# A graph kernel whose first sweep closes its rows with fixed weights and turns the results on VectorE

## The chip, the cores and the metric

One core of a Trainium2 chip. The time is what the device takes for one run of the program, in microseconds (us). TensorE (PE in the profile) multiplies, VectorE (DVE) adds and transposes, ScalarE (ACT) applies tanh and square root, GpSimd (POOL) and SyncE (SP) mostly issue transfers.

## What is computed

`adj` is a dense 8192 x 8192 float32 matrix, `x` is 8192 x 64. Four layers follow one another, each `x = x + layer(relu(layernorm(x)))`; the first has two hops, so that `adj` is multiplied five times:

```python
# layer 0, two hops: sweeps 1 and 2
for k in range(2):
    h = tanh(concatenate([adj @ h, h], axis=1) @ W[k])
# layer 1: sweep 3        adj @ (h @ weight) + bias
# layer 2: sweep 4        adj @ (h * (u >= 0.1) / 0.9)
# layer 3: sweep 5        concatenate([h, adj @ h / (deg + 1)]) @ W.T,  deg = sum(adj, axis=1)
```

The change is about layer 0. There `h` enters each hop twice: through `adj @ h` and, as the row's own features, beside it. The tanh of hop 1 is what hop 2 sweeps over, and is also hop 2's own features.

## The kernel before, in words

**Blocks and sweeps.** `adj` is cut into 16 x 16 blocks of 512 x 512 (1 MB each). A sweep makes, for each of the 16 rows i of blocks, the sum over j of block (i, j) times the features of nodes j. Since five sweeps would read the matrix five times, most blocks are used for two sweeps at one load: block (i, j) serves sweep s for row i and, as the features of nodes j for sweep s + 1 are already there, sweep s + 1 for row i too. Odd sweeps sum in partitions 0 to 63 (`row.half` 0), even ones in 64 to 127; `two_products` (L747) multiplies for both, `one_product` (L720) for one, splitting the 512 nodes of the row into two halves of 256 columns that stand in the two halves of the partitions. In the lists, sweep 1 goes down from row 0 to row 15; row i takes its blocks j > i and then j = i singly ("single"), and j = i - 2 and i - 1 as "double" at its end. Further, as soon as the features of nodes i - 1 exist for sweep 2, the blocks (k, i - 1) of all rows k > i + 1 are taken as "early" groups between the single blocks of row i. In the kernel before they start after the third single block of a row (after the fourth in row 1); where a row has too few, those left over stand behind its last single block. Rows 1 to 6 end with one more block of sweep 2 ("late"). Sweep 2 goes up from row 15 to row 0, and begins with a few late blocks before its short rows.

**The order of work** is one list, `PLAN`, written by `make_plan` (L122): "block", "first" and "doubles" (VectorE takes the sums of the single and double blocks from PSUM), "turn" (a row's own features are brought from nodes by partition to features by partition), "post" (a row is closed), "added" and "added_both" (a late or early group is added to `partial`). Every engine walks through the same list in order and does its part, with semaphores between them. SyncE loads blocks through a ring of 8 in the order of the list.

**Closing a row ("post").** `stack` holds, by features, 64 partitions of sums and 64 of own features, for 512 nodes. In `post` (L782) TensorE multiplies it with the 128 x 64 weights in `w_stack`: 8 products, in each of which 64 nodes of `stack` are the fixed operand and the 64 columns of the weights are streamed (L814). The results in `natural` have nodes by partition. ScalarE's tanh (L909) writes them in sweep 1 straight into `operand`, which is what sweep 2 multiplies with, and in sweep 2 into `tanh_out`, from which VectorE's `finish` makes the next layer's features, square root on ScalarE (L853) and operand (L1158) among it. In sweep 1 the post of row i - 1 stands after row i's second single block (after its only one in row 15).

**Turns.** In sweeps 1, 2 and 5 VectorE's `turn_in_squares` (L1011) transposes own features from `operand` into `stack` with 8 transposes of 32 partitions x 128 (L1028). Row 15 of sweep 2 is turned by TensorE (L779).

**Sums.** `take_first` (L1051) and `take_doubles` (L1084) bring a row's sums into `stack` (L1074, L1093); in sweep 1 `take_doubles` then also adds the other sweep's half to `partial` (L1009). In sweeps 2 to 4 that half is saved by a copy on ScalarE (L893) at "doubles". The next row but one that uses a sum bank waits for these.

**Degrees.** VectorE adds up `adj` for the row sums `deg`: two additions of 128 x 1024 for each block in `DEGREE_BLOCKS` (L989, L990; the first block of a row has one, L986) and a fold of three instructions at the end of a row (L994, L997, L1001). In sweep 1 all single blocks of rows 9 to 15 are among them, of rows 0 to 8 only the diagonal one, and the double blocks of rows 1 and 2; in sweep 2 the double blocks of rows 0 to 8. A ring slot is free only when its block has been added (L693).

Of the kernel before, what the change touches and what calls it, by code (L numbers as in the profile page):

```python
# [36 lines left out]
F = 64  # L37
P = 128
BLOCK = 512
NB = N // BLOCK  # L40
TPB = BLOCK // P
SQUARE = 32
# [58 lines left out]
ROW_OF = {(row.sweep, row.i): row for row in ROWS}  # L101


class Block:


# [4 lines left out]
def make_plan():  # L111
# [36 lines left out]
    def row_of(row, post_at, hoisted=False, between=None):  # L148


        n_single = 0 if hoisted else len(row.single)
        total = n_single + len(row.double)
        before = [("post", ROWS[row.r - 1])] if row.r % NB or row.sweep == SWEEPS else []
        if row.double:
            post_at = min(post_at, total - 1)
        at = {n: [] for n in range(total + 1)}
        if n_single == 0:
            at[0].append(("first", row))
        if row.own:
            at[min(1, n_single)].append(("turn", row))  # L160
        at[min(post_at, total)] += before
        for n in range(1, total + 1):
            at[n] += between(row.i, n) if between else []
        if row.sweep == 4 and row.i == DEGREES_AT:
            at[min(2, total)].append(("degree", row))
        if n_single:
            at[n_single].insert(0, ("first", row))
        if row.double:
            at[total].append(("doubles", row))
            if n_single:  # L170
                blocks(row, row.single, "single", {n: at[n] for n in range(n_single)})
            blocks(row, row.double, "double", {n - n_single: at[n] for n in range(n_single, total + 1)})
        else:
            blocks(row, row.single, "single", at)

    def upwards(sweep, between=None):
# [30 lines left out]
        for i in range(NB - 2, -1, -1):  # L207
            row = ROW_OF[sweep, i]
            if i >= NB - 4:

                plan.append(("first", row))
                turning = [("turn", row)] if row.own else []
                if i == NB - 2:
                    plan.extend(turning)
                if i < NB - 2 and fills[NB - i]:
                    takings = fill_with(fills[NB - i], False)
                    plan.append(("post", ROWS[row.r - 1]))
                    plan.extend(takings)
                    plan.extend(turning)
                    if i == NB - 3:  # L220
                        fill_with(fills[NB - i + 1])
                    blocks(row, row.double, "double")
                else:
                    blocks(row, row.double, "double", {1: [("post", ROWS[row.r - 1])] if i < NB - 2 else []})
                plan.append(("doubles", row))
            else:
                row_of(row, 1, between=between)
# [8 lines left out]
    for row in ROWS[:NB]:  # L236
        groups = [(k, [row.i - 1]) for k in range(row.i + 2, NB)] if row.i else []
        at_first = min(1, len(row.single) - 1)
        begin = 3 if row.i == 1 else 2
        starts = [min(begin + c, len(row.single) - 1) for c in range(len(groups))]  # L240
        for n, j in enumerate(row.single):
            plan.append(("block", Block(count[0], row, j, "single", n == 0, n == len(row.single) - 1)))
            count[0] += 1
            if n == (at_first if row.r else NB // 2):
                if row.r:
                    plan.append(("post", ROWS[row.r - 1]))
                plan.append(("turn", row))
# [202 lines left out]

def rows_in_squares(r):

    return sum(row.own and not turned_by_tensor(row) for row in ROWS[: r + 1])


def added_to(row):
# [71 lines left out]
def gnn_kernel(nc, adj, x, w_both, w_own, bias, u, identity, ones, out):  # L528
# [5 lines left out]
    with ctx:  # L534
# [93 lines left out]
        tanh_ready = sem("tanh_ready")  # L628
        sd_ready = sem("sd_ready")

        weights_cleared = sem("weights_cleared")

        def data_of(b):
# [25 lines left out]
        def wait_operand(wait_ge, sweep, j):  # L659
# [1 line left out]
            if sweep == 1:  # L661
                wait_ge(first_ready, j * TPB // GROUP + 1)
            elif sweep == 2:
                wait_ge(tanh_ready, ROW_OF[1, j].r + 1)
            else:
                wait_ge(norm_ready, ROW_OF[sweep - 1, j].r + 1 - NB)

# [40 lines left out]
        def _(pe):  # L708
# [73 lines left out]
            def post(row):  # L782
# [11 lines left out]
                    wait_new(later_consts, 16 * LATER_CONSTS)  # L794
                if turned_by_tensor(row):
                    wait_new(own_ready, rows_with_own(row.r))
                elif row.own:
                    wait_new(squares_ready, rows_in_squares(row.r))
                if row.r >= 2:
# [3 lines left out]
                    else:  # L803
                        wait_new(natural_taken, before.r + 1 - 2 * NB)
                acc = natural[row.r % 2]
                stacked = partial[:, row.i, :] if row.sweep == SWEEPS else stack[:, row.r % 2, :]
                for t in range(TPB):
                    if row is ROWS[-1] and t == TPB // 2:
                        last.then_inc(half_posted, 1)
                        wait_new(first_taken, rows_with_first(row.r))  # L810
# [35 lines left out]
        def _(act):  # L846
            deviations = [0]

            def deviation(n, slot):
# [2 lines left out]
                act.wait_ge(var_ready, deviations[0])  # L852
                nc.scalar.activation(sd[:, slot, 0:n], moments[:, slot, 0:n, 1], ACT.Sqrt, bias=eps[:, 0:1]).then_inc(sd_ready, 1)  # L853

            def scale_own(row):

                wait_operand(act.wait_ge, row.sweep, row.i)
# [25 lines left out]
            for g in range(2, NGROUPS):  # L883
                deviation(GROUP, g % 2)
            for what, row in PLAN:
                if what in ("block", "added", "added_both"):
                    continue
                slot = row.r % 2
                if what == "doubles" and row.sweep > 1:

                    act.wait_ge(blocks_used, used(row, "double"))
                    other = half_of(1 - row.half)
                    nc.scalar.copy(partial[other, row.i, :], double_acc[slot][other, :]).then_inc(partial_saved, 1)  # L893
                elif what == "scale" or what == "turn" and row.sweep == SWEEPS and row is not ROWS[-1]:
                    scale_own(row)
                elif what == "turn" and turned_by_tensor(row):
# [5 lines left out]
                elif what == "post":  # L902
                    if row.r == CONSTS_AT:
                        load_constants()
                    if row.sweep <= 2:
                        act.wait_ge(posted, posts(row.r))
                        got = natural[slot][:, 0:TPB * F].rearrange("p (t f) -> p t f", t=TPB)
                        to = operand[:, tiles(row.i), F:2 * F] if row.sweep == 1 else tanh_out[:, slot]
                        nc.scalar.activation(to, got, ACT.Tanh).then_inc(tanh_ready, 1)  # L909
                    if row.sweep in (2, 3, 4):  # L910
                        deviation(TPB, 0)
                    if row.sweep == SWEEPS:
# [14 lines left out]
        def _(dve):  # L927
# [111 lines left out]
            def turn_back(row):  # L1039
# [8 lines left out]
                last.then_inc(turned_back, 1)  # L1048
                dve.wait_ge(turned_back, rows_turned_back(row.r))

            def take_first(row):  # L1051


# [25 lines left out]
            def take_doubles(row):  # L1079
# [4 lines left out]
                    dve.wait_ge(first_taken, rows_with_first(row.r))  # L1084
                    before = stack[part, row.r % 2, :]
                else:
                    wait_stack(row)
                    wait_partial(dve.wait_ge, row)
                    if added_to(row):
                        dve.wait_ge(added_taken, added_to(row))  # L1090
                    dve.wait_ge(blocks_used, used(row, "double"))
                    before = partial[part, row.i, :]
                last = nc.vector.tensor_tensor(stack[part, row.r % 2, :], got[part, :], before, ALU.add)  # L1093
                last.then_inc(sums_ready, 1)
                if row.sweep == 1:
                    add_to(partial[other, row.i, :], got[other, :], ("doubles", row.r, row.sweep + 1) in FRESH)\
# [90 lines left out]
            for what, of in PLAN:  # L1187
# [7 lines left out]
                elif what == "first":  # L1195
                    take_first(of)
                    if of.r == 2 * NB:
                        make_folding()
                elif what == "doubles":
                    take_doubles(of)  # L1200
                elif what == "added":
# [48 lines left out]
```

## Time and profile before

| | |
|---|---|
| median of 3 runs | 2269.01 us (2268.98 to 2269.06) |
| the profiled execution | 2268.98 us |
| its span | 2267.2 us |
| PE, DVE, ACT busy | 2241.6, 1253.2, 116.4 us |
| share of PE in the chain that ended last | 97% |
| adjacency loads | 780 of 1 MB |
| granted TensorE clock | full in every slice |

The span is the time from the first to the last instruction of the profiled execution; 1.78 us of its time lie outside. Instructions are named by line and engine; a busy share of PE is modelled, since matmuls are pipelined, and a group's duration reaches beyond the start of the next by its drain. So PE's work is best read from start to start. One product in float32 shows as two matmul records with a weight load each: a single block is 16 of them with 256 columns, a double block 16 with 512.

### The profile page before, as it was taken

Reading aid. Unit: us, or ns where it says so; the run is one execution under the profiler, and the core shown is the slowest. Engines: PE = TensorE matmul, PEld = TensorE weight load, DVE = VectorE, ACT = ScalarE, POOL = GpSimd, SP = SyncE. Lnnn points to the kernel's source line nnn. Section 1 sums busy time; section 2 is a strip of 40 time slices with the busy share of each in tenths; the row PEclk is TensorE's granted clock in tenths of the full one; section 3 lists DMA queues with packets and bytes.
Section 4 is the critical chain, followed back from the end, with each engine's and each line's share of the span. In section 5 each row is a group of like instructions: output and inputs, shape, how many; then the busy total and the mean of one; then the engine's idle time right before and its main releaser. Section 6 shows DMA issues by size and latency. Waiting matters only on the chain.

```text
span 2267.2 us, 32808 instructions
## 1 busy us (share of the span) xinstructions
PE 2241.6 (99%) x13886; PEld 1073.9 (47%) x13886; DVE 1253.2 (55%) x2612; ACT 116.4 (5%) x240; POOL 9.6 (0%) x22
## 2 busy tenths in 40 slices
PE   6999999999999999999999999999999999999999
PEld 3555555555555444444454444444444444444446
DVE  7133222224777399987889888877534322222226
ACT  1000000000002211100100000000000000000000
POOL 0000000000000000000000000000000000000000
PEclk9999999999999999999999999999999999999999
DMA  9999999999999878788888888886999999999998
GB/s 398 421 421 412 405 399 397 385 385 398 397 404 375 292 285 324 298 305 304 354 310 333 320 322 323 316 338 251 351 369 409 406 408 409 404 409 407 404 408 325
DMA packets 117010, 826.56 MB, mean 365 GB/s; under 512 B 13824, under 2 KB 16128, under 8 KB 16896
## 3 DMA queue, kind: packets, MB, share of 16 engines
q1 hardware_dynamic: 112752, 820.04, 91.5%
q0 software_dynamic: 768, 2.10, 0.3%
q10 hardware_dynamic: 3344, 2.33, 0.3%
q8 instruction: 110, 1.80, 0.3%
q14 instruction: 36, 0.29, 0.0%
HBM read 822.31 MB, written 2.10 MB: 364 GB/s over the span
## 4 chain that ended last, share of the span: by engine, by line
PE 97%; DMA 2%; DVE 0%; SPq 0%; issue 0%; ACT 0%; DVEq 0%
PE double_acc L751 59%; PE single_acc L725 17%; PE spare L751 14%; PE spare L725 6%; DMA ring<-in_adj 2%; PE natural L814 1%; DVE partial L1009 0%; SPq L695 0%; PE spare L826 0%; DVE resid L1176 0%; SPq L688 0%; DVE centred L953 0%; DVE partial L1074 0%; DVE stats L941 0%; PE spare L779 0%
## 5 line engine op out<-in xcount | busy, mean ns | idle before, releaser
L751 PE MATMUL double_acc<-ring,operand 128*64 128x512 f32 x6176 | 1350.5, 592 | 0.2
L751 PEld LDWEIGHTS double_acc<-ring,operand 128*64 128x64 f32 x6176 | 501.3, 137 | 766.5 <-issue 751.3
L725 PE MATMUL single_acc<-ring,operand 128*64 128x256 f32 x3472 | 411.2, 381 | 20.7 <-DVE operand L967 11.9
L1009 DVE TENSOR_TENSOR partial<-spare,partial 64x256 f32<-64x256 f32 (+1 forms) x204 | 107.0, 525 | 495.6 <-PE spare L751 273.5
L725 PEld LDWEIGHTS single_acc<-ring,operand 128*64 128x64 f32 x3472 | 277.4, 138 | 171.7 <-issue 75.7
L751 PE MATMUL spare<-ring,operand 128*64 128x512 f32 x1456 | 330.3, 592 | 0.6 <-DMA ring<-in_adj 0.6
L990 DVE TENSOR_TENSOR deg_part<-deg_part,ring 128x1024 f32<-128x1024 f32 x215 | 263.4, 1225 | 7.4
L989 DVE TENSOR_TENSOR deg_part<-deg_part,ring 128x1024 f32<-128x1024 f32 x215 | 263.2, 1224 | 6.4
L751 PEld LDWEIGHTS spare<-ring,operand 128*64 128x64 f32 x1456 | 125.7, 137 | 149.2 <-issue 141.5
L1009 DVE TENSOR_TENSOR partial<-single_acc,partial 64x256 f32<-64x256 f32 x118 | 49.8, 422 | 174.7 <-PE single_acc L725 172.7
L725 PE MATMUL spare<-ring,operand 128*64 128x256 f32 x1152 | 134.3, 379 | 0.0
L725 PEld LDWEIGHTS spare<-ring,operand 128*64 128x64 f32 x1152 | 84.7, 137 | 59.7 <-issue 27.9
L893 ACT COPY partial<-double_acc 64x512 f32<-64x512 f32 x45 | 26.1, 579 | 1195.3 <-PE double_acc L751 1195.3
L1028 DVE STREAM_TRANSPOSE stack<-operand 32x128 f32<-32x128 f32 x248 | 75.0, 303 | 3.9
L1093 DVE TENSOR_TENSOR stack<-double_acc,partial 64x512 f32<-64x512 f32 x39 | 26.9, 691 | 84.0 <-PE double_acc L751 83.5
L1093 DVE TENSOR_TENSOR stack<-double_acc,stack 64x512 f32<-64x512 f32 x21 | 14.3, 683 | 92.1 <-PE double_acc L751 91.9
L953 DVE TENSOR_SCALAR centred<-resid,moments,rsd 128x64 f32<-128x64 f32 x256 | 62.9, 310 | 2.3
L1008 DVE COPY partial<-spare 128x512 f32<-128x512 f32 (+1 forms) x15 | 9.8, 656 | 63.7 <-PE spare L751 60.1
L941 DVE BATCH_NORM_STATS2 stats<-resid 128x6 f32<-128x64 f32 x256 | 38.6, 214 | 6.0 <-DMA resid<-in_x 4.4
L814 PEld LDWEIGHTS natural<-w_stack,stack 128*64 128x64 f32 x816 | 35.1, 138 | 12.9 <-issue 9.8
L1028 DVE STREAM_TRANSPOSE partial<-scaled 32x128 f32<-32x128 f32 x128 | 38.9, 304 | 2.1
L909 ACT ACTIVATE operand<-natural 128x256 f32<-128x256 f32 x16 | 6.1, 383 | 646.3 <-PE natural L814 646.3
(67 smaller groups left out, 579.5 us busy)
## 6 DMA issues: line engine op xcount, KB each, us to landing
ring<-in_adj SPq DMA_DIRECT2D x766, 1024.0 KB, 7.4
held<-in_adj SPq DMA_DIRECT2D x12, 1024.0 KB, 10.0
kept<-in_adj SPq DMA_DIRECT2D x2, 1024.0 KB, 12.7
for_layer<-in_u POOLq DMA_DIRECT2D x16, 128.0 KB, 2.4
out_rows<-resid ACTq DMA_DIRECT2D x15, 128.0 KB, 6.7
resid<-in_x SPq DMA_DIRECT2D x2, 512.0 KB, 6.0
resid<-in_x SPq DMA_DIRECT2D x1, 1024.0 KB, 13.7
out_rows<-resid ACTq DMA_DIRECT2D x2, 64.0 KB, 1.7
```

Source lines behind the costliest of these rows:

```text
L725: last = nc.tensor.matmul(acc[half_of(h), 0:HALF], operand[:, b.j * TPB + t, half_of(b.row.half)], stream[:, t, nodes_of(h)], start=b.firs ...
L751: last = nc.tensor.matmul(acc[half_of(half), :], operand[:, b.j * TPB + t, half_of(half)], stream[:, t, :], start=b.first and t == 0, stop ...
L814: last = nc.tensor.matmul(acc[half_of(c), t * F:(t + 1) * F], stacked[:, nodes], w_stack[:, row.sweep - 1, :], start=True, stop=True)
L893: nc.scalar.copy(partial[other, row.i, :], double_acc[slot][other, :]).then_inc(partial_saved, 1)
L941: last = nc.vector.bn_stats(stats[:, slot, t, :], values[:, t, :])
L953: last = nc.vector.tensor_scalar(centred[:, t, :], values[:, t, :], moments[:, slot, t, 0:1], rsd[:, t:t + 1], ALU.subtract, ALU.mult)
L989: link(nc.vector.tensor_tensor(acc, acc, data[:, 0:2 * BLOCK], ALU.add))
L990: nc.vector.tensor_tensor(acc, acc, data[:, 2 * BLOCK:], ALU.add).then_inc(deg_added, 1)
L1008: return nc.vector.tensor_copy(to, got)
L1009: return nc.vector.tensor_tensor(to, got, to, ALU.add)
L1028: last = nc.vector.transpose(to[:, :, part], own[part, :, c * SQUARE:(c + 1) * SQUARE])
L1093: last = nc.vector.tensor_tensor(stack[part, row.r % 2, :], got[part, :], before, ALU.add)
```

## The change

What it does, in sweep 1 for rows 0 to 14 (`turned_home`) and in sweep 2 for the same rows (`with_home`):

- `post` in sweep 1 makes 2 products instead of 8: the weights are fixed, and 256 nodes of `stack` are streamed in each. The result has features by partition.
- Two tanh of 64 x 256 write it into `partial`, partitions 0 to 63 of the row, beside sweep 2's sums.
- VectorE's new `turn_home` (a new entry "home" in the list, behind "post") transposes it from there into `operand`, with 8 transposes, and sets `home_ready`. Whoever multiplies with sweep 2's features waits for that instead of for tanh.
- In sweep 1 the post stands after the first single block of the next row, not the second; every row's early groups begin after the fourth single block, not the third.
- In sweep 2 these rows have no "turn": their own features lie in `partial` already. `take_doubles` adds the sums to `partial` in place, and `post` reads `partial`. The copy of the other half (`save_next`) would overwrite the own features, so ScalarE makes it after the row's tanh and before its square root.

```diff
@@ make_plan, sweep 1
-        begin = 3 if row.i == 1 else 2
+        begin = 3
...
+            if n == 0 and row.r:
+                plan.append(("post", ROWS[row.r - 1]))
+                plan.append(("home", ROWS[row.r - 1]))
             if n == (at_first if row.r else NB // 2):
-                if row.r:
-                    plan.append(("post", ROWS[row.r - 1]))
                 plan.append(("turn", row))
@@ row_of and upwards
-        if row.own:
+        if row.own and not with_home(row):
...
@@ wait_operand
             elif sweep == 2:
-                wait_ge(tanh_ready, ROW_OF[1, j].r + 1)
+                if j < NB - 1:
+                    wait_ge(home_ready, j + 1)
+                else:
+                    wait_ge(tanh_ready, NB)
@@ post, TensorE
-                stacked = partial[:, row.i, :] if row.sweep == SWEEPS else stack[:, row.r % 2, :]
-                for t in range(TPB):
+                stacked = partial[:, row.i, :] if row.sweep == SWEEPS or with_home(row) else stack[:, row.r % 2, :]
+                if turned_home(row):
+                    for h in range(2):
+                        last = nc.tensor.matmul(acc[half_of(h), 0:HALF], w_stack[:, 0, :], stacked[:, nodes_of(h)], start=True, stop=True)
+                for t in range(0 if turned_home(row) else TPB):
@@ ScalarE
+            def save_next(row):
+
+                other = half_of(1 - row.half)
+                nc.scalar.copy(partial[other, row.i, :], double_acc[row.r % 2][other, :]).then_inc(partial_saved, 1)
...
+                    if turned_home(row):
+                        act.wait_ge(posted, posts(row.r))
+                        for h in range(2):
+                            last = nc.scalar.activation(partial[half_of(0), row.i, nodes_of(h)], natural[slot][half_of(h), 0:HALF], ACT.Tanh)
+                        last.then_inc(tanh_ready, 1)
...
+                    if with_home(row):
+                        save_next(row)
                     if row.sweep in (2, 3, 4):
                         deviation(TPB, 0)
@@ VectorE
+            def turn_home(row):
+
+                dve.wait_ge(tanh_ready, row.r + 1)
+                for c in range(F // SQUARE):
+                    results = partial[c * SQUARE:(c + 1) * SQUARE, row.i, :].rearrange("p (t n) -> p t n", t=TPB)
+                    for q in range(QUARTERS):
+                        part = slice(q * SQUARE, (q + 1) * SQUARE)
+                        last = nc.vector.transpose(operand[part, tiles(row.i), F + c * SQUARE:F + (c + 1) * SQUARE], results[:, :, part])
+                last.then_inc(home_ready, 1)
...
-                last = nc.vector.tensor_tensor(stack[part, row.r % 2, :], got[part, :], before, ALU.add)
+                stacked = partial[part, row.i, :] if with_home(row) else stack[part, row.r % 2, :]
+                last = nc.vector.tensor_tensor(stacked, got[part, :], before, ALU.add)
```

## Rows read from the trace of the kernel before

**Rows 1.** The page: busy time of the engines; chain that ended last, by engine.

```profile
PE 2241.6 (99%) x13886; PEld 1073.9 (47%) x13886; DVE 1253.2 (55%) x2612; ACT 116.4 (5%) x240; POOL 9.6 (0%) x22
...
PE 97%; DMA 2%; DVE 0%; SPq 0%; issue 0%; ACT 0%; DVEq 0%
```

**Rows 2.** Chain in order of time, mid-sweep 2: start us, us, what.

```profile
873.07 34.34 PE double_acc L751 x160
907.41 0.47 PE natural L814 x16
907.87 12.41 PE double_acc L751 x57
```

**Rows 3.** Windows: busy us (instructions) by engine, then granted clock, DMA share, GB/s.

```profile
640.00:692.00 52.00, 52.00 (x346) 26.97 (x344) 43.84 (x75) 1.15 (x3) 0.00 (x0) 1.00 0.99 401
800.00:900.00 100.00, 100.00 (x511) 41.06 (x508) 94.77 (x140) 11.47 (x15) 0.00 (x0) 1.00 0.81 310
```

**Rows 4.** PE's waits from 57 to 760 us; from 80 us on none: total, times, longest.

```profile
PE spare L751 <- DMA ring<-in_adj: 0.6, 1, 0.6
PE single_acc L725 <- DMA ring<-in_adj: 0.5, 1, 0.5
```

**Rows 5.** Timeline of PE, sweep 1, rows 13 and 15: start us, us, what.

```profile
656.31 3.65 PE L725 MATMUL single_acc<-ring,operand 128*64 128x256 f32 x32
659.76 0.66 PE L814 MATMUL natural<-w_stack,stack 128*64 128x64 f32 x16
660.23 1.93 PE L725 MATMUL single_acc<-ring,operand 128*64 128x256 f32 x16
...
685.24 7.07 PE L751 MATMUL double_acc<-ring,operand 128*64 128x512 f32 x32
```

**Rows 6.** Timeline of DVE, sweep 1, rows 13 to 15; in brackets the idle time before.

```profile
656.55 0.68 DVE L1093 TENSOR_TENSOR stack<-double_acc,stack 64x512 f32<-64x512 f32 x1 [4.17 <-PE double_acc L751]
...
657.99 1.23 DVE L986 TENSOR_TENSOR deg_part<-ring 128x1024 f32<-128x1024 f32 x1
659.25 1.23 DVE L989 TENSOR_TENSOR deg_part<-deg_part,ring 128x1024 f32<-128x1024 f32 x1
...
661.77 2.53 DVE L1028 STREAM_TRANSPOSE stack<-operand 32x128 f32<-32x128 f32 x8
...
672.50 0.68 DVE L1093 TENSOR_TENSOR stack<-double_acc,stack 64x512 f32<-64x512 f32 x1 [2.01 <-PE double_acc L751]
...
683.42 0.68 DVE L1093 TENSOR_TENSOR stack<-double_acc,stack 64x512 f32<-64x512 f32 x1
...
684.86 1.23 DVE L986 TENSOR_TENSOR deg_part<-kept 128x1024 f32<-128x1024 f32 x1
...
688.31 2.53 DVE L1028 STREAM_TRANSPOSE stack<-operand 32x128 f32<-32x128 f32 x8
...
692.34 0.68 DVE L1093 TENSOR_TENSOR stack<-double_acc,stack 64x512 f32<-64x512 f32 x1 [0.61 <-PE double_acc L751]
```

**Rows 7.** Timeline of ACT: a tanh of sweep 1, the turn's copies, a saved half.

```profile
660.47 0.38 ACT L909 ACTIVATE operand<-natural 128x256 f32<-128x256 f32 x1 [20.72 <-PE natural L814]
...
698.42 0.74 ACT L900 COPY stack<-spare 64x256 f32<-64x256 f32 x2 [3.51 <-PE spare L779]
...
709.23 0.58 ACT L893 COPY partial<-double_acc 64x512 f32<-64x512 f32 x1 [6.38 <-PE double_acc L751]
```

**Rows 8.** Timeline of PE: sweep 1, rows 2 and 11; sweep 2, row 13.

```profile
131.71 3.65 PE L725 MATMUL single_acc<-ring,operand 128*64 128x256 f32 x32
...
624.91 3.63 PE L751 MATMUL spare<-ring,operand 128*64 128x512 f32 x16
...
712.91 7.07 PE L751 MATMUL double_acc<-ring,operand 128*64 128x512 f32 x32
```

**Rows 9.** Timeline of DVE: sweep 1, row 1's sums; sweep 2, row 14's operand.

```profile
132.85 0.68 DVE L1093 TENSOR_TENSOR stack<-double_acc,stack 64x512 f32<-64x512 f32 x1
...
714.91 0.29 DVE L1158 TENSOR_SCALAR operand<-centred 128x256 f32<-128x256 f32 x1
```

More of the change, by code:

```diff
@@ L101, with turned_home, with_home @@
 ROW_OF = {(row.sweep, row.i): row for row in ROWS}
+def turned_home(row):
+    return row.sweep == 1 and row.i < NB - 1
+def with_home(row):
+    return row.sweep == 2 and row.i < NB - 1
 class Block:
@@ L211, in upwards @@
                 plan.append(("first", row))
-                turning = [("turn", row)] if row.own else []
+                turning = [("turn", row)] if row.own and not with_home(row) else []
                 if i == NB - 2:
@@ L451, in rows_in_squares @@
 def rows_in_squares(r):
-    return sum(row.own and not turned_by_tensor(row) for row in ROWS[: r + 1])
+    return sum(row.own and not turned_by_tensor(row) and not with_home(row) for row in ROWS[: r + 1])
 def added_to(row):
@@ L629, in gnn_kernel @@
         sd_ready = sem("sd_ready")
+        home_ready = sem("home_ready")
         weights_cleared = sem("weights_cleared")
@@ L796, in post @@
                     wait_new(own_ready, rows_with_own(row.r))
+                elif with_home(row):
+                    wait_new(tanh_ready, row.i + 1)
                 elif row.own:
@@ L885, in _ @@
             for what, row in PLAN:
-                if what in ("block", "added", "added_both"):
+                if what in ("block", "added", "added_both", "home"):
                     continue
                 slot = row.r % 2
-                if what == "doubles" and row.sweep > 1:
+                if what == "doubles" and row.sweep > 1 and not with_home(row):
                     act.wait_ge(blocks_used, used(row, "double"))
-                    other = half_of(1 - row.half)
-                    nc.scalar.copy(partial[other, row.i, :], double_acc[slot][other, :]).then_inc(partial_saved, 1)
+                    save_next(row)
                 elif what == "scale" or what == "turn" and row.sweep == SWEEPS and row is not ROWS[-1]:
@@ L904, in _ @@
                         load_constants()
-                    if row.sweep <= 2:
+                    if turned_home(row):
[3 more added lines that the diff above has]
+                        last.then_inc(tanh_ready, 1)
+                    elif row.sweep <= 2:
                         act.wait_ge(posted, posts(row.r))
@@ L909, in _ @@
                         nc.scalar.activation(to, got, ACT.Tanh).then_inc(tanh_ready, 1)
+                    if with_home(row):
+                        save_next(row)
                     if row.sweep in (2, 3, 4):
@@ L1086, in take_doubles @@
                 else:
-                    wait_stack(row)
+                    if not with_home(row):
+                        wait_stack(row)
                     wait_partial(dve.wait_ge, row)
@@ L1198, in _ @@
                         make_folding()
+                elif what == "home":
+                    turn_home(of)
                 elif what == "doubles":
```

## The prediction

> **What bounds the kernel now.** I read the page first. TensorE (PE) is busy for 99% of the span and VectorE (DVE) for 55%; PE also makes up 97% of the chain that ended last [rows 1]. A busy PE in this profile is a modelled one, so I went on to the chain in order of time. In the middle of sweep 2, ten double blocks take 34.34 us (3.434 each), a row's closing product 0.47, and the next double block follows at once [rows 2]. There is nothing between products there, although VectorE is 94.77 of 100 us busy in the same stretch [rows 3]. PE's waits between 57 and 760 us are two waits for loads, 0.6 and 0.5 us, both in the first 23 us of that stretch [rows 4]. So from 80 us on at the latest the end is set by PE alone: time taken off another engine is worth nothing, and every microsecond in which PE waits goes straight to the end, because no later wait is there to swallow it.
>
> The profiled execution took 2268.98 us against a span of 2267.2, so 1.78 us lie outside; it agrees with the median of 2269.01 within 0.03. I forecast on its span and add 1.78. A measurement here can tell about 0.2%, or 4.5 us, from no change.
>
> **Part 1: the closing product itself, 15 rows of sweep 1.** Before, 8 products of 64 columns, each recorded in two passes, run as 16 weight loads and 16 matmuls; start to start with what follows, this takes 660.23 - 659.76 = 0.46 us [rows 5]. The new form is not in the trace. Its 2 products of 256 columns are 4 recorded matmuls of just the shape of a single block's, and 32 of those take 659.76 - 656.31 = 3.45 us [rows 5], so 4 take 0.43. The other end is the 0.66 us that the old form occupies with its drain [rows 5]. I take 0.43, the same shape. The gain is 0.03 x 15 = 0.45 us; by the other end it is a loss of 3 us (0.20 x 15, counted from 0.46). Two passes over 256 columns are streamed either way: only weight loads go, and they were under the stream.
>
> **Part 2: tanh.** ScalarE did one 128x256 activation, starting 0.71 us after the product began and lasting 0.38 [rows 5, 7]. It now does two of 64x256; two copies of that shape took 0.74 [rows 7]. I take 0.70 + 0.76 (ends 0.38 and 0.77 for the second term), so tanh is complete 1.46 us after the product begins.
>
> **Part 3: the turns.** VectorE loses 15 x 8 transposes in sweep 2 and gains 15 x 8 in sweep 1, of one shape: 2.53 us for 8, 2.56 with their spacing [rows 6]; the strided side is the output instead of the input, and I allow 2.4 to 3.0. In sweep 2 the 38 us saved are worth nothing [rows 2, 3]. In sweep 1 a turn home now lies between tanh and the first product that uses the new features, and everything behind it in VectorE's queue (degree sums, the own turn, the sums that the next closing product needs) moves back by 2.56 us.
>
> **Part 4: the post one block earlier.** It comes one single block (1.73 us) after a row's double blocks rather than two. VectorE adds the sums 0.24 us after the last double block and needs 0.69, so 0.8 us of margin is left where VectorE is not late [rows 5, 6]. Row 1 is a small exception: its sums end at 132.85 + 0.68 = 133.53, and row 2's first single block starts at 131.71, so that the post is now due at 133.44 [rows 8, 9]: 0.1 us. The groups that begin one block later, at the fourth single block, have their home turn in time: it ends 5.8 us after the row's start, they are due at 7.35. No load is late for it, since PE no longer waited for loads by then [rows 4].
>
> **Part 5: the crowded end of sweep 1.** In rows 9 to 15 VectorE adds degrees for each single block (two instructions of 1.23, 1.26 apart, so 2.52 us [rows 6] against PE's 1.73), while the rows shrink. I write the new queue on the old clock. *Row 11* has three groups and now two of them behind the last single block; the third reuses the bank of the first. Measured from the row's start, VectorE goes: sums and saved half to 1.70, first degree add to 2.94, home 3.23 to 5.76 (tanh is complete at 1.73 + 1.46), block 2 to 8.3, own turn to 10.84, blocks 3 and 4 to 15.88, taking of group 1 to 16.57. PE is there at 15.95 (five single blocks, the product and two groups of 3.43; on the old clock 624.9, where the third group started before too [rows 8]). Cost 0.6 to 0.7. *Row 13*, PE from 656.31: post at 658.04, tanh complete 659.50, home 659.54 to 662.07; the group that needs it is due at 661.93, so 0.2 us, hidden or not. What matters is VectorE's own chain. It took 672.50 - 656.55 = 15.95 with 2.01 idle, so 13.94 of work [rows 6]; with home 2.56 and 0.29 of waiting for tanh, row 13's sums start at 673.34, 0.84 late. *Row 14* was already solid VectorE work, 683.42 - 672.50 = 10.92 [rows 6]; it becomes 13.48, and its sums run 686.82 to 687.51. *Row 15* begins on PE at about 683.3, one single block, and its post (of row 14) is due at 685.0 but waits for these sums: **first wait, 2.5 us**. Then VectorE does the saved half, the last degree add and the fold (684.86 to 688.31 is 3.45 for add and fold [rows 6]; with the sum's 0.71 and the saved half's 0.73 it is 4.89) and only then home, 691.71 to 694.24. PE starts the first double block at 687.9 and wants block 14 at 691.4; **second wait, 2.9 us**. Block 14 of the last row starts at 694.4 and did at 685.24 + 3.43 = 688.67 [rows 5]: 5.7 us later.
>
> **Part 6: sweep 2.** The copy of the other half (0.58 us [rows 7]) moves behind tanh, ahead of the square root. So the operand of row 14, finished at 714.91 + 0.29 = 715.20, is finished 0.6 later, and PE wants it at 712.91 + 3.43 = 716.34 [rows 8, 9]: hidden with 0.5 to spare. If that cover is gone it costs that row some tenths. The end of sweep 2 has a like margin. The sum bank, freed by that copy, is next wanted two rows later, and the copy ends some 2 us after the post that stands in the first half of the row between: no wait.
>
> **The sum.** -0.45 (posts) + 0.1 (row 2) + 0.65 (row 11) + 5.75 (rows 13 to 15, net of the three posts' 0.09, which are counted already, hence +0.09) = 6.1. Span 2273.3, time 2275.1. With every unknown at its good end (home 2.4, tanh 0.38, row 11 just in time) it is +4.6; with the bad ends (home 3.0 three times in the solid chain, 1.3 us; post 0.66, 3.4 us) it is +10.8.
>
> **Where a rule speaks otherwise.** The whole old post fits in 0.46 us with its 16 weight loads [rows 5]. The Trainium skill (TensorE: Matmul & The Clock Gate, What overlaps and what doesn't) lets a weight load run beside matmuls only in other rows of the array, and its formula for 64 columns (LDWEIGHTS) would make an estimated 53 ns each, 12 of them fewer per post: 9.6 us gained over 15 rows. By that rule the trace disagrees: 16 such loads alone would outlast the post.
>
> **The rivals.**
> *The cover holds, wholly or in part* (the change does nothing measurable). VectorE's slack in rows 13 to 15 is larger than I read, say because a wait in its old chain shows as none. For it: PE never waited there [rows 4]. Against: 10.92 us without a gap [rows 6]. Without any wait, -0.45: 2268.6; with one of the two waits of row 15, 2271.5 to 2273.
> *The weight loads did cost PE time* (the other side: faster). Place: the 15 posts. If 12 of 16 loads gone take three quarters of 0.46 along, that is 0.35 x 15 = 5.2 us; with the waits of part 5 absent the time is 2263.8. It decides only if the waits stay below 0.7 us altogether. Against it: a single block with as many loads per matmul streams at just its columns' rate [rows 5].
> *PE's clock falls in the two waits.* The granted clock is 1.00, the level of 2.4 GHz, in mid-sweep 2 and in the crowded end of sweep 1 alike [rows 3], and no wait after 80 us exists to show what 2.5 to 3 us idle do. At 1.2 instead of 2.4 GHz a double block takes 6.87 instead of 3.43, so one or two blocks cost 3.4 to 6.9 more: 2278.5 to 2282. The Trainium skill's same page (HAM oscillation) has the clock halved by idle gaps between bursts; no row here shows it.
>
> **How the numbers follow.** Forecast 0.66 (own range 2273.7 to 2277.5), cover 0.20, faster 0.04, clock 0.10. The first and the last are slower by over 0.2%: 0.76; the cover case is within 0.2%: 0.20. The range 2270.5 to 2280 leaves out the faster case, about half of the cover case and half of the clock case.
>
> **What would show it.** Right: PE waits for the sums (VectorE, L1093's line) before row 14's post and for home before the last double block, 2 to 3 us each; VectorE without idle time from row 13 to the end of sweep 1; sweep 2 shifted by about 6 us and its row pitch unchanged; closing products 0.43. Wrong: no PE wait between 640 and 700 us; a post of 0.2 or 0.6; a granted clock below 1.00; waits spread over rows 3 to 10 (post too early) or at row 14 of sweep 2 (square root too late).

## The result and the profile after

The changed kernel takes 2275.36 us (median of 9 runs, 2275.24 to 2276.9), the kernel before 2269.05 in runs between them: ratio 1.0029, interval 1.0019 to 1.0038, so 6.3 us slower. The forecast was 2275.1 in a range of 2270.5 to 2280. The profiled execution took 2275.28 with a span of 2273.5, 6.3 above the span before.

The page: busy time of the engines, and the chain that ended last by engine.

```profile
PE 2242.7 (99%) x13706; PEld 960.1 (42%) x13706; DVE 1254.0 (55%) x2612; ACT 120.3 (5%) x255; POOL 9.6 (0%) x22
...
PE 95%; DVE 2%; DMA 2%; issue 0%; ACT 0%; DVEq 0%; ACTq 0%
```

Against [rows 1], TensorE has 180 matmuls fewer (15 rows, 16 to 4) and VectorE exactly as many instructions as before, with a busy time 0.8 us longer: nothing was saved there in sum, work was moved. What is new is VectorE with 2% in the chain.

PE's waits from 80 to 2240 us: engine, line, who was waited for, total, times, longest. Before there was none: [rows 4] says so up to 760 us, and the same view of the kernel before lists none from 760 us to the end.

```profile
PE double_acc L766 <- DVE operand L1088: 2.5, 1, 2.5
PE natural L826 <- DVE stack L1135: 2.5, 1, 2.5
PE spare L766 <- DVE partial L1039: 0.6, 1, 0.6
```

L1088 is the turn home, L1135 the sums of the double blocks, L1039 the taking of a group. The same stretches in time, first PE and then VectorE (start us, us, what; in brackets the idle time before). The first four lines of PE are the closing product of row 10 and row 11's groups, the others row 15.

```profile
610.59 0.60 PE L826 MATMUL natural<-stack,w_stack 128*64 128x256 f32 x4
611.02 5.35 PE L740 MATMUL single_acc<-ring,operand 128*64 128x256 f32 x48
...
621.36 3.60 PE L766 MATMUL spare<-ring,operand 128*64 128x512 f32 x16
625.61 3.65 PE L766 MATMUL spare<-ring,operand 128*64 128x512 f32 x16 [0.64 <-DVE partial L1039]
...
683.97 1.90 PE L740 MATMUL single_acc<-kept,operand 128*64 128x256 f32 x16
688.37 0.65 PE L826 MATMUL natural<-stack,w_stack 128*64 128x256 f32 x4 [2.50 <-DVE stack L1135]
688.85 3.60 PE L766 MATMUL double_acc<-ring,operand 128*64 128x512 f32 x16
694.96 3.65 PE L766 MATMUL double_acc<-ring,operand 128*64 128x512 f32 x16 [2.50 <-DVE operand L1088]
```

```profile
657.24 0.68 DVE L1135 TENSOR_TENSOR stack<-double_acc,stack 64x512 f32<-64x512 f32 x1 [0.94 <-PE double_acc L766]
...
660.27 2.51 DVE L1088 STREAM_TRANSPOSE operand<-partial 32x128 f32<-32x128 f32 x8 [0.37 <-ACT partial L931]
...
674.16 0.68 DVE L1135 TENSOR_TENSOR stack<-double_acc,stack 64x512 f32<-64x512 f32 x1
...
687.63 0.68 DVE L1135 TENSOR_TENSOR stack<-double_acc,stack 64x512 f32<-64x512 f32 x1
...
689.07 1.23 DVE L1016 TENSOR_TENSOR deg_part<-kept 128x1024 f32<-128x1024 f32 x1
...
692.41 2.50 DVE L1088 STREAM_TRANSPOSE operand<-partial 32x128 f32<-32x128 f32 x8
```

Read the brackets first. The sums that used to wait for PE (2.01 idle before the one at 672.50 [rows 6]) now have no bracket: from 657.24 on, VectorE has 0.37 us of idle time until row 15's home turn (all of it ahead of the turn at 660.27), so it is what sets the pace. PE's brackets stand in row 15. The listed 2.50 is counted from the modelled end of the matmul before; from start to start, row 15's single block (1.73) should have been followed at 685.70 and the product came at 688.37, 2.67 later, and block 14's double block at 694.96 instead of 688.85 + 3.43 = 692.28, 2.68 later.

Mid-sweep 2 in windows (busy us by engine, then granted clock, DMA share, GB/s), and the chain there:

```profile
800.00:900.00 100.00, 100.00 (x510) 34.44 (x508) 87.60 (x116) 11.14 (x15) 0.00 (x0) 1.00 0.81 302
```

```profile
879.38 34.34 PE double_acc L766 x160
913.72 0.46 PE natural L834 x16
```

VectorE fell from 94.77 to 87.60 us here [rows 3], and ten double blocks take 34.34 us as before [rows 2]: relief that nobody waited for.

### The profile page after: what moved, and what is told of

Its sections match the earlier page's. It is cut to its first block, busy times and chain, and to the rows that moved or that the text cites. A ratio compares the mean times of both kernels' runs of the same rounds, so it can differ in the third digit from the quotient of the medians.

```text
span 2273.5 us, 32437 instructions
## 1 busy us (share of the span) xinstructions
PE 2242.7 (99%) x13706; PEld 960.1 (42%) x13706; DVE 1254.0 (55%) x2612; ACT 120.3 (5%) x255; POOL 9.6 (0%) x22
## 4 chain that ended last, share of the span: by engine, by line
PE 95%; DVE 2%; DMA 2%; issue 0%; ACT 0%; DVEq 0%; ACTq 0%
PE double_acc L766 58%; PE single_acc L740 17%; PE spare L766 13%; PE spare L740 6%; DMA ring<-in_adj 2%; PE natural L834 1%; DVE operand L1088 0%; DVE deg_part L1019 0%; DVE deg_part L1020 0%; DVE stack L1058 0%; PE natural L826 0%; DVE partial L1039 0%; DMA resid<-in_x 0%; DVE centred L983 0%; DVE deg_part L1016 0%
## 5 line engine op out<-in xcount | busy, mean ns | idle before, releaser
L766 PEld LDWEIGHTS double_acc<-ring,operand 128*64 128x64 f32 x6176 | 441.9, 137 | 828.2 <-issue 808.9
L1039 DVE TENSOR_TENSOR partial<-spare,partial 64x256 f32<-64x256 f32 (+1 forms) x204 | 107.0, 525 | 460.6 <-PE spare L766 238.0
L740 PEld LDWEIGHTS single_acc<-ring,operand 128*64 128x64 f32 x3472 | 254.7, 138 | 192.4 <-issue 75.8
L766 PEld LDWEIGHTS spare<-ring,operand 128*64 128x64 f32 x1456 | 107.9, 137 | 172.8 <-issue 161.9
L1039 DVE TENSOR_TENSOR partial<-single_acc,partial 64x256 f32<-64x256 f32 x118 | 49.8, 422 | 174.7 <-PE single_acc L740 172.7
L740 PEld LDWEIGHTS spare<-ring,operand 128*64 128x64 f32 x1152 | 82.4, 137 | 61.9 <-issue 28.0
L1135 DVE TENSOR_TENSOR stack<-double_acc,stack 64x512 f32<-64x512 f32 x21 | 14.3, 683 | 85.2 <-PE double_acc L766 84.9
L1135 DVE TENSOR_TENSOR partial<-double_acc,partial 64x512 f32<-64x512 f32 x15 | 10.4, 694 | 68.6 <-PE double_acc L766 68.6
L931 ACT ACTIVATE partial<-natural 64x256 f32<-64x256 f32 x30 | 11.4, 380 | 636.0 <-PE natural L826 635.9
L1088 DVE STREAM_TRANSPOSE operand<-partial 32x128 f32<-32x128 f32 x120 | 36.2, 302 | 15.5 <-ACT partial L931 14.0
L1058 DVE STREAM_TRANSPOSE stack<-operand 32x128 f32<-32x128 f32 x128 | 39.0, 304 | 2.1
```

The lines of the kernel that those rows point to most:

```text
L740: last = nc.tensor.matmul(acc[half_of(h), 0:HALF], operand[:, b.j * TPB + t, half_of(b.row.half)], stream[:, t, nodes_of(h)], start=b.firs ...
L766: last = nc.tensor.matmul(acc[half_of(half), :], operand[:, b.j * TPB + t, half_of(half)], stream[:, t, :], start=b.first and t == 0, stop ...
L1039: return nc.vector.tensor_tensor(to, got, to, ALU.add)
L1058: last = nc.vector.transpose(to[:, :, part], own[part, :, c * SQUARE:(c + 1) * SQUARE])
L1088: last = nc.vector.transpose(operand[part, tiles(row.i), F + c * SQUARE:F + (c + 1) * SQUARE], results[:, :, part])
L1135: last = nc.vector.tensor_tensor(stacked, got[part, :], before, ALU.add)
```

## The experiments

The kernel before ran beside each; its medians lay between 2268.99 and 2269.03.

**1. The new places alone, on the kernel before.** Closing product, tanh and turns stay.

```diff
-        begin = 3 if row.i == 1 else 2
+        begin = 3
...
+            if n == 0 and row.r:
+                plan.append(("post", ROWS[row.r - 1]))
             if n == (at_first if row.r else NB // 2):
-                if row.r:
-                    plan.append(("post", ROWS[row.r - 1]))
```

> The kernel before with the new places only: post after the first single block, every row's early groups after the fourth; the product, tanh and turns stay as they were. My theory (VectorE's home turn makes the waits, the places don't): only row 2's post comes 0.1 to 0.15 us before its sums, 2269.15 us (2269.0 to 2269.4), no wait of TensorE in rows 11 to 15. Rival (the post one block earlier makes the waits): 2274 to 2276, with a wait before the post of row 14.

Measured 2269.45 (2269.33 to 2269.54), 0.45 above before, and no wait in rows 11 to 15. Row 2's product starts 1.88 us after the single block ahead of it, not 1.73, as it had to:

```profile
131.78 1.93 PE L725 MATMUL single_acc<-ring,operand 128*64 128x256 f32 x16
133.66 0.69 PE L814 MATMUL natural<-w_stack,stack 128*64 128x64 f32 x16
134.18 5.35 PE L725 MATMUL single_acc<-ring,operand 128*64 128x256 f32 x48
```

The product itself then takes 0.52 instead of 0.46. That makes 0.21 of the 0.45. The rest is the same thing once more, in sweep 2, though no wait is listed for it: row 14's product starts 1.94 us after the single block ahead of it and takes 0.52, which is 0.27 more than the two took before (709.00 to 711.19).

```profile
709.28 1.90 PE L725 MATMUL single_acc<-ring,operand 128*64 128x256 f32 x16
711.22 0.69 PE L814 MATMUL natural<-w_stack,stack 128*64 128x64 f32 x16
711.74 1.90 PE L725 MATMUL spare<-ring,operand 128*64 128x256 f32 x16
...
711.22 0.55 PEld L814 LDWEIGHTS natural<-w_stack,stack 128*64 128x64 f32 x16 [0.50 <-DVE stack L1093]
```

The last line is that product's weight loads. They waited for VectorE's sums and start together with the product, where before they started 0.12 us ahead of it (710.60 against 710.72). Why VectorE's sums are late there (710.47, 0.62 later than before, while TensorE is 0.28 later) stays open; the changed kernel has no such loss at this place. The one wait that the view lists for this kernel from 80 to 2240 us, 0.2 before a double block at 1604.09, is no loss: from the single blocks to that double block it is 3.78 us here and 3.77 before. So the places alone cost half a microsecond; the 6.3 come only with the turn home.

**2. The old places under the change.**

```diff
-        begin = 3
+        begin = 3 if row.i == 1 else 2
...
-            if n == 0 and row.r:
+            if n == at_first and row.r:
```

> The changed kernel with the old places: post and home after the second single block, early groups after the third. My theory: home ends 7.5 us after a row's start (8.0 in rows 9 to 13, behind two degree adds), the first group is due at 5.6, so TensorE waits 1.9 in each of rows 2 to 8 and 2.4 in rows 9 to 13, then 2.9 in row 14 and 2.2 in row 15, and the old waits go: about 2300 us (2295 to 2305). Rival (only the crowded end counts, the places matter little): 2272 to 2278.

Measured 2301.65 (2300.7 to 2305.78), as expected. PE waits for home 12 times before a group, 22.9 us in all and at most 2.2, and twice before double blocks:

```profile
PE spare L766 <- DVE operand L1088: 22.9, 12, 2.2
PE double_acc L766 <- DVE operand L1088: 4.4, 2, 2.6
```

So the places are not what costs the 6.3 us but what keeps them from being more: under the change they are worth some 25 us (2300.70 against 2275.28 in the profiled executions). The falls of the clock that follow the waits are part of that; the four runs read a mean clock of 0.997 to 0.999, and the profiled one shows one fall, at 602 us.

**3 and 4. Row 15's degree sums behind home.** In the changed kernel row 15's degree add and fold (3.45 us) stand ahead of the home turn that PE's last double block needs. Both kernels hold them back, the first until row 15's own turn is made (the diff below), the second until its sums are (the same two lines behind `take_doubles`).

```diff
                 if what == "block":
-                    if of in DEGREE_BLOCKS:
+                    if of in DEGREE_BLOCKS and of is not HELD_BACK:
                         add_degrees(DEGREE_BLOCKS.index(of), of)
...
                     turn_in_squares(of, range(F // SQUARE - 1) if of is ROWS[-1] else range(F // SQUARE))
+                    if of is ROWS[NB - 1]:
+                        add_degrees(DEGREE_BLOCKS.index(HELD_BACK), HELD_BACK)
```

> The changed kernel; row 15's degree add and fold (3.45 us) are made behind its home and own turn instead of ahead of home. My theory: the second wait (before block 14's last double block) shrinks from 2.7 to about 0.25, but row 15's own sums are 3.45 later and its post waits 2.4: the time stays, 2275.4 us (2274.8 to 2276). Rival (the second wait is home's own latency behind tanh): the second wait stays at 2.7 and a third is added, 2277.8.

Measured 2276.94 (2276.92 to 2277.05), above the expected range. The waits came as the theory said: none is listed for home, and 2.3 us for row 15's sums stand in its place.

```profile
PE natural L827 <- DVE stack L1136: 2.5, 1, 2.5
PE natural L835 <- DVE stack L1136: 2.3, 1, 2.3
PE spare L767 <- DVE partial L1040: 0.6, 1, 0.6
```

The 1.5 us that the expectation missed are TensorE's clock. Windows of this kernel, columns as above:

```profile
695.00:700.00 5.00, 2.93 (x22) 1.29 (x18) 4.72 (x8) 0.00 (x0) 0.00 (x0) 1.00 0.90 338
700.00:705.00 5.00, 4.77 (x40) 3.03 (x42) 2.56 (x6) 0.39 (x1) 0.00 (x0) 0.66 0.17 48
```

The second row's granted clock is 0.66, a mean of the two levels 2.4 and 1.2 GHz, right behind the second wait. The two single blocks in it start 2.55 and 2.59 us apart:

```profile
700.23 0.69 PE L835 MATMUL natural<-w_stack,stack 128*64 128x64 f32 x16 [2.30 <-DVE stack L1136]
700.75 2.78 PE L741 MATMUL spare<-ring,operand 128*64 128x256 f32 x16
703.30 2.75 PE L741 MATMUL single_acc<-kept,operand 128*64 128x256 f32 x16
705.89 0.61 PE L795 MATMUL spare<-ident,operand 128*64 128x128 f32 x8
```

That is 5.14 instead of 3.45, 1.7 us lost. All four runs read a mean clock of 0.999.

> The changed kernel; row 15's degree add and fold are made behind its sums. My theory: the second wait shrinks from 2.7 to 0.25 and no third takes its place but for up to 0.6 us where sweep 2's first late groups are taken: 2273.5 us (2272.8 to 2274.0), first wait unchanged at 2.7. Rival (home's latency behind tanh): 2275.4.

Measured 2274.25 as a median, but the ten runs fall into two groups: five from 2273.50 to 2273.58, in all of which the mean granted clock of the run reads 1.000, and five from 2274.92 to 2275.14, in which it reads 0.999. The first group, to which the profiled execution belongs, is the expected 2273.5. The second I take for the same with one fall of the clock, 1.5 us; there is no trace of it, and only the mean clock says so.

```profile
PE natural L827 <- DVE stack L1136: 2.5, 1, 2.5
PE spare L767 <- DVE partial L1040: 0.7, 1, 0.7
PE spare L795 <- DVE partial L1040: 0.3, 1, 0.3
```

The wait for home is gone from the list and a wait of 0.3 before sweep 2's turn by TensorE has come, so 1.8 us are won in the first group. With the degree sums out of its way home ends in time but for 0.2 us (the two double blocks of row 15 take 7.07 us from start to start instead of 6.87): what PE waited for was VectorE's queue and, beyond these 0.2, not tanh or the transposes themselves.

**5. Degree sums of rows 12 to 14 later.** All but the diagonal blocks of these rows are added in sweep 2.

```diff
-DEGREES_LATER = (0, 1, 2, 3, 4, 5, 6, 7, 8)
+DEGREES_LATER = (0, 1, 2, 3, 4, 5, 6, 7, 8, 12, 13, 14)
```

> The changed kernel with the degree adds of rows 12, 13 and 14 (all but their diagonal blocks) moved from sweep 1's single blocks to sweep 2's double blocks. My theory (a solid VectorE chain from row 13 on makes the first wait): VectorE is idle again in rows 12 and 13, the first wait shrinks from 2.7 to about 1.0, the second (home behind row 15's degree add and fold) stays at 2.7 to 2.9: 2273.8 us (2273.2 to 2274.3). Rival (the wait is the post's place or tanh): 2275.4.

Measured 2279.23 (2278.63 to 2279.59): a miss by 5.4 us. The crowded end did what was expected (first wait 0.8, second 2.5), but two new waits stand in sweep 2:

```profile
PE natural L834 <- DVE partial L1135: 3.0, 2, 2.4
PE double_acc L766 <- DVE operand L1088: 2.5, 1, 2.5
PE natural L826 <- DVE stack L1135: 0.8, 1, 0.8
PE spare L766 <- DVE partial L1039: 0.6, 1, 0.6
```

Sweep 2's rows 14 and 13 have one and two double blocks, and their add and fold now lie between these blocks and their sums. I had looked at VectorE's idle time in sweep 2, not at what stands in its queue behind the adds. Most of the rest is the clock again: all four runs read 0.999, and the profiled one has a fall at 730 us, right behind the wait of 2.4; the four double blocks that follow take 15.27 us instead of 13.74.

**6. Both moves, row 11 too.** Row 15's degree sums behind its sums as in 4, and

```diff
-DEGREES_LATER = (0, 1, 2, 3, 4, 5, 6, 7, 8)
+DEGREES_LATER = (0, 1, 2, 3, 4, 5, 6, 7, 8, 11, 12, 13, 14)
```

> The changed kernel with the degree adds of rows 11 to 14 later and row 15's behind its sums. My theory: row 11's wait of 0.6 goes, the first wait is 1.0, the second 0.2, up to 0.6 is lost at sweep 2's first groups: 2271.3 us (2270.6 to 2272.0). Rival (waits that only move): 2273 to 2275.

Measured 2276.9 (2275.98 to 2277.12), above the expected range and the rival's too, by the same cause: four waits of 4.2 us in all for sweep 2's sums, and the clock (1.000 in the run of 2275.98, the profiled one, and 0.999 in the others).

```profile
PE natural L835 <- DVE partial L1136: 4.2, 4, 2.4
```

**7. The home turn twice.** The 8 transposes are made again behind the first 8.

```diff
+                for again in range(2):
-                for c in range(F // SQUARE):
+                    for c in range(F // SQUARE):
...
+                    if again == 0:
+                        link(last)
```

> The changed kernel with each home turn made twice (same data again). My theory: home ends 8.35 us after a row's start instead of 5.8, the first group is due at 7.35, so each of rows 2 to 12 waits 1.0; rows 9 to 11 wait some 2.4 more in all where a bank is reused, and the chain from row 12 to 15 grows by 8.3: about +21.5, 2297 us (2293 to 2301). Rival (home is covered outside rows 13 to 15): +8, 2283.

Measured 2300.04 (2297.39 to 2303.31), within the range and above the expected 2297 by about what the clock adds: these runs read 0.996 to 0.999, and the profiled one (2299.06) has two falls. Row 3's group shows the cover that one turn has and two have not:

```profile
209.70 5.35 PE L740 MATMUL single_acc<-ring,operand 128*64 128x256 f32 x48
215.83 3.65 PE L766 MATMUL spare<-ring,operand 128*64 128x512 f32 x16 [0.78 <-DVE operand L1089]
```

The group starts 0.95 us behind the three single blocks' 5.18, as against the expected 1.0. Twelve groups wait 11.8 us in all, and PE waits 11.1 us more for the double blocks' homes, for sums and for banks.

**8. Sweep 2's turns kept.** `turn` stays in the list for these rows and VectorE transposes into the `stack` that nobody reads.

```diff
-        if row.own and not with_home(row):
+        if row.own:
...
-                if F // SQUARE - 1 in features:
+                if F // SQUARE - 1 in features and not with_home(row):
                     last.then_inc(squares_ready, 1)
```

> The changed kernel with sweep 2's own turns of rows 0 to 14 still made by VectorE, into the stack that nobody reads then (38 us of VectorE work put back). My theory (VectorE's relief in sweep 2 is worth nothing, TensorE sets the pace): 2275.4 us (2275.2 to 2275.8). Rival (the relief did help and hid a larger loss): slower by 2 us or more.

Measured 2275.33 (2275.24 to 2275.71), the time of the changed kernel within 0.03. VectorE is 94.78 us busy from 800 to 900 us again:

```profile
800.00:900.00 100.00, 100.00 (x510) 34.34 (x508) 94.78 (x140) 11.13 (x15) 0.00 (x0) 1.00 0.80 304
```

Some 36 us of VectorE work (120 transposes of 0.30) in sweep 2 are worth nothing, put in or taken out. This trace also shows a fall of the clock that cost nothing: it came between the two waits, the double block took 5.3 us, and the second wait shrank from 2.5 to 0.8. The next double block starts 6.11 us after it, as in the changed kernel (694.96 - 688.85). The first line is a window, columns as above.

```profile
690.00:695.00 5.00, 4.34 (x14) 1.11 (x10) 4.80 (x12) 0.03 (x1) 0.00 (x0) 0.68 0.74 308
...
689.04 5.30 PE L766 MATMUL double_acc<-ring,operand 128*64 128x512 f32 x16
695.15 3.65 PE L766 MATMUL double_acc<-ring,operand 128*64 128x512 f32 x16 [0.81 <-DVE operand L1088]
```

**9. The change only where it is covered**, rows 0 and 2 to 9 (`HOME`), each with its new places; the others as before.

```diff
+HOME = (0, 2, 3, 4, 5, 6, 7, 8, 9)
...
-    return row.sweep == 1 and row.i < NB - 1
+    return row.sweep == 1 and row.i in HOME
...
-        begin = 3
+        begin = 3 if row.i == 1 or row.r and turned_home(ROWS[row.r - 1]) else 2
```

> The change made only in rows 0 and 2 to 9, where home's turn has room; rows 1 and 10 to 14 keep the old product, turn, post and places. My theory: no wait of TensorE after 80 us, and 9 closing products of 0.43 instead of 0.46: 2268.8 us (2268.6 to 2269.0), 0.25 below the kernel before. Rival (the fixed weights bring nothing at all): 2269.05.

Measured 2268.88 (2268.83 to 2269.05) against 2269.03 (2268.92 to 2269.26): 0.15 less, with an interval of the ratio of 0.999 to 1.0008. That is no difference one could claim. The theory's "no wait" holds but for one listed wait of 0.2, which is the one of experiment 1 and no loss: 3.78 us against 3.77 before.

**10. The adds left out instead of moved.** As 6, but those of rows 11 to 14 are not made in sweep 2 either.

```diff
-    or b.row.sweep == 2 and b.kind == "double" and b.row.i in DEGREES_LATER
+    or b.row.sweep == 2 and b.kind == "double" and b.row.i < 9
```

> As the run with both moves, but the degree adds taken from rows 11 to 14 of sweep 1 are left out and not made in sweep 2, so the degrees of these rows leave those blocks out. My theory (the earlier miss of the two runs with later degrees is only new waits in sweep 2's short rows, where the sums of rows 14 to 11 now stand behind degree adds): those waits go, row 11's too, the first wait is 0.8 to 1.0, the second at most 0.1, and 0.3 to 0.5 is lost at sweep 2's turn by TensorE: 2271.2 us (2270.8 to 2271.6); runs in which the clock falls after a wait 1.5 more. Rival (moving the adds cost something else): 2273 or more.

Measured 2270.88 (2270.69 to 2271.03), 0.3 below the expected value and in its range; the waits of sweep 2 are gone, 0.8 and 0.3 are left, and all ten runs read a clock of 1.000.

```profile
PE natural L827 <- DVE stack L1136: 0.8, 1, 0.8
PE spare L795 <- DVE partial L1040: 0.3, 1, 0.3
```

With row 15's fold moved and 24.7 us less VectorE work in rows 11 to 14 (1254.0 to 1229.3 us busy), 4.5 of the 6.3 us are back. So what moving the adds cost in 5 and 6 was the new waits, and the falls of the clock that came with them; with these waits gone, none of the ten runs shows a fall.

**11. Row 11 as well.**

```diff
-HOME = (0, 2, 3, 4, 5, 6, 7, 8, 9)
+HOME = (0, 2, 3, 4, 5, 6, 7, 8, 9, 11)
```

> As the run with the change in rows 0 and 2 to 9, and in row 11 too: its home turn falls into row 12, where VectorE had 0.9 us to spare in the changed kernel. My theory: still no wait, one closing product more of 0.43: 2268.85 us (2268.75 to 2268.95), the fastest of all. Rival (row 12's late VectorE delays row 13's sums): 2269.2 to 2270.

Measured 2268.66 (2268.57 to 2268.76, 11 runs) against 2268.99 (2268.91 to 2269.12, 20 runs). That is faster than the expected range by 0.09. No run of one reaches into the other's, and PE has no wait after 80 us, but the ratio's interval, 0.9989 to 1.0008, holds 1: it is the lowest time of all, 0.33 us below the kernel before, which a measurement here doesn't tell from no change. The trace shows where it comes from: row 2 starts at 131.73 against 131.71 before, row 13 at 656.02 against 656.31. Nine of the new closing products lie between, 0.03 us each.

## Why the prediction was right

It named the mechanism, the place and, within 0.3 us, the size; that the size came out so close is in part luck, as errors of 0.1 to 0.2 in its terms have opposite signs. By its parts:

- **Closing product.** Forecast 0.43; measured 611.02 - 610.59 = 0.43. Row 3 started at 206.14 before and at 206.34 after, row 11 at 608.94 and 608.86, so the eight products between had won 0.28 us: 0.035 each. The weight loads that went had cost PE next to nothing, and the rival that lived on them is out. Behind a wait the new product takes 0.48.
- **Tanh and turn.** Two tanh took 0.77 (forecast 0.76) and the turn 2.51 (2.53), strided output or not.
- **Row 2.** Forecast 0.1; it was 0.15 for the wait (1.88 us after the single block) and 0.05 for a product of 0.48.
- **Rows 3 to 10.** Forecast no wait, and none came: row 3's home turn ended 5.7 us after the row's start (forecast 5.8) and its group began at 7.3 (7.35).
- **Row 11.** Forecast 0.65; the third group started at 625.61 instead of 621.36 + 3.43 = 624.79, so 0.8: undersized by 0.15.
- **Rows 13 to 15.** VectorE's chain through row 13 was forecast at 13.94 + 2.56 + 0.29 = 16.79 and took 674.16 - 657.24 = 16.92, that through row 14 at 13.48 and 687.63 - 674.16 = 13.47. The two waits were forecast at 2.5 and 2.9 and were 2.67 and 2.68; from row 14's sums to home it took 692.41 - 687.63 = 4.78 against 4.89. Together 5.35 against 5.4. Row 13's 0.2 was 662.84 - 662.62 = 0.22. (The forecast's own sum is loose here: 694.4 - 688.67 + 0.09 is 5.82 and not 5.75; its 6.1 stays.)
- **Sweep 2.** Relief worth nothing: experiment 8. The square root was to make row 14's operand 0.6 later; against PE it came 0.2 later (721.47 against 714.91, where PE's double blocks of row 13 had moved from 712.91 to 719.25). The step was oversized, since the root had had time to spare: before, it waited 0.25 us for VectorE's statistics, and after, it followed its table load without a wait. It was hidden either way.
- **The clock.** I gave it one in ten as a rival and priced it at 3.4 to 6.9 us, one or two double blocks at half speed. That price was at least twice too high: a fall cost 1.5 to 1.7 us when it fell on work and nothing when it fell into a wait. Nor is it a rival, but an addition that comes in some executions. In the changed kernel one run of nine, 2276.9, seems to have carried it (there is no trace of it); three others that read 0.999 are as fast as those that read 1.000, which fits the trace of experiment 8. The Trainium skill (TensorE: Matmul & The Clock Gate, HAM oscillation) says that idle gaps between bursts of products bring the halved clock; the traces of experiments 3 and 8 agree, with 0.66 and 0.68 in the windows behind a wait.

What I did not foresee is in the fixes, not in the forecast: that degree adds moved to sweep 2 would put waits there, ahead of its short rows' sums (experiments 5 and 6).

## What to carry to other kernels

Where one engine works without a gap, a change that only moves work between other engines can't win, and loses where the moved piece enters a chain that was already solid and that this engine waits for; write out the receiving engine's queue, instruction by instruction, at its tightest stretch. Idle time in a stretch is not room: what counts is what stands in the queue behind the new piece and when it is due, and a piece taken out of one crowd must be followed to the next. A new dependency can be paid for by its place in the order: here two single blocks' more distance, one ahead of the post's old place and one behind the groups', was worth some 25 us.

## What the runs showed of the hardware

- The granted clock fell to its lower level after waits of 2.2 to 2.5 us (traces of experiments 2, 3, 5 and 8), in some executions of a kernel and not in others: the profiled ones of the changed kernel and of experiments 4 and 6 have such waits and no fall. By the mean clock it fell in five of ten runs of experiment 4, whose times lie in two groups 1.5 us apart, and in all four of experiment 3. The kernels without such a wait (before, experiments 1, 9, 10 and 11) read 1.000 in every run that stood beside the experiments or in them.
- The busy time of the weight loads tells nothing about the time here. The kernel before shows 1073.9 us [rows 1]; experiment 1, with the same 13886 loads and 0.45 us more time, shows

```profile
PE 2242.3 (99%) x13886; PEld 958.1 (42%) x13886; DVE 1253.7 (55%) x2612; ACT 116.3 (5%) x240; POOL 9.6 (0%) x22
```

  Experiments 9 and 11, which have no wait in row 2, are back at 1074.1 and 1070.4. So the lower figure goes with an early wait, the matmuls' pace stays, and what ties the two is not shown.
- Two products of 256 columns with fixed weights and eight of 64 columns with changing ones cost 0.43 and 0.46 us: in float32 with 64 weight columns, 12 weight loads more were worth 0.03 us.
